# Norms of batches 0 and 1 by halves, and new orders of the engines, in a graph network on one core

## The reference

```
x = norm(x + adj @ (x @ W) + b)                                    # L0
x = norm(x + L1(x))      # ((si + sj' + adj * wr + gb) @ x) @ W + b, si = x.wi, sj = x.wj
x = norm(x + L2(x))      # attention: sigmoid(a_tgt + a_src + be) * mask(adj), times elu(x @ Wi + bi)
for _ in range(5):       # L3: gated unit, h = x at the start
    m  = adj @ h
    z  = sigmoid(m @ W3 + h @ U3 + ..); r = sigmoid(m @ W4 + h @ U3 + ..)
    h  = (1 - z) * h + z * tanh(m @ W5 + (r * h) @ U5 + ..)
x = norm(x + h)
```

## Time and profile before

| | us |
|---|---|
| median of 3 runs (1234.6 to 1240.07) | 1237.77 |
| the profiled execution | 1235.95 |
| its span, first to last instruction | 1234.0 |
| TensorE busy | 1172.3 |
| DVE busy | 927.5 |
| ScalarE busy | 684.7 |
| GpSimd busy | 74.5 |

### The profile page before, as it was taken

One profiled execution on the slowest core, in us unless ns is written; L12 is line 12 of the kernel. 1 busy time (PEld: TensorE's weight loads), 2 busy tenths in 40 slices (PEclk: granted clock), 3 DMA queues, 4 the chain that ended last, 5 costly groups with the idle time before them and its releaser, 6 DMA issues.

```text
span 1234.0 us, 15530 instructions
## 1 busy us (share of the span) xinstructions
PE 1172.3 (95%) x5232; PEld 907.4 (74%) x5232; DVE 927.5 (75%) x2071; ACT 684.7 (55%) x1119; POOL 74.5 (6%) x80
## 2 busy tenths in 40 slices
PE   7979899799999999999999999999999999999995
PEld 5866368577777878877777677887777768788884
DVE  5987986588878886677887886685798788554656
ACT  4336762666566675356567565546457657544443
POOL 0110010000000011001000001000001002000001
PEclk9999999899999999999999999999999999999997
DMA  7222330132222322121232322211332322000001
GB/s 249 87 76 94 102 112 1 34 120 78 94 94 85 95 86 88 41 77 60 92 96 78 128 94 69 69 52 52 104 111 86 111 78 86 18 1 1 1 1 35
DMA packets 92575, 93.66 MB, mean 76 GB/s; under 512 B 9104, under 2 KB 62992, under 8 KB 92496
## 3 DMA queue, kind: packets, MB, share of 16 engines
q1 hardware_dynamic: 92352, 92.27, 23.0%
q0 software_dynamic: 144, 0.40, 0.1%
HBM read 65.35 MB, written 27.29 MB: 75 GB/s over the span
## 4 chain that ended last, share of the span: by engine, by line
PE 58%; DVE 22%; ACT 6%; issue 4%; DMA 4%; SPq 4%; POOL 2%; DVEq 0%; POOLq 0%; ACTq 0%
PE ps L813 33%; PE ps L818 4%; PE ps L820 4%; PE ps L819 4%; PE ps L936 4%; DVE ring L1544 3%; PE ps L831 3%; ACT x L1133 3%; DMA mk<-mask_scratch 2%; SPq L693 2%; DVE tl L1359 2%; DVE hT L1598 1%; DVE v L1595 1%; PE ps L824 1%; DVE ml L1359 1%
## 5 line engine op out<-in xcount | busy, mean ns | idle before, releaser
L813 PE MATMUL ps<-adj_hi,xh 128*128 128x512 f32 x672 | 281.6, 419 | 13.1 <-DVE xl L1359 7.1
L813 PE MATMUL ps<-adj_hi,xl 128*128 128x512 f32 x672 | 263.0, 391 | 0.0
L813 PE MATMUL ps<-adj_lo,xh 128*128 128x512 f32 x672 | 262.5, 391 | 0.0
L813 PEld LDWEIGHTS ps<-adj_hi,xh 128*128 128x128 f32 x672 | 126.7, 189 | 50.4 <-issue 19.0
L813 PEld LDWEIGHTS ps<-adj_lo,xh 128*128 128x128 f32 x672 | 126.8, 189 | 32.6 <-issue 8.9
L813 PEld LDWEIGHTS ps<-adj_hi,xl 128*128 128x128 f32 x672 | 126.4, 188 | 27.3
L1577 DVE TENSOR_TENSOR r<-r,hT 128x512 f32<-128x512 f32 x80 | 53.7, 688 | 76.8 <-ACT r L1271 76.8
L818 PE MATMUL ps<-mh,wh 128*128 128x512 f32 x240 | 101.9, 425 | 6.7 <-DVE ml L1359 5.2
L1544 DVE TENSOR_TENSOR ring<-ring,mk 128x512 f32<-128x512 f32 x128 | 86.9, 685 | 27.2 <-ACT ring L1206 23.9
L1206 ACT ACTIVATE ring<-fh,asn 128x512 f32<-128x512 f32 x96 | 67.3, 719 | 62.6 <-DVE mk L1359 21.5
L1128 ACT ACTIVATE mh<-ps 128x512 fp32r<-128x512 f32 x80 | 47.2, 590 | 92.0 <-PE ps L813 92.0
(11 more groups left out here) (295 smaller groups left out, 2374.2 us busy)
## 6 DMA issues: line engine op xcount, KB each, us to landing
mk<-mask_scratch SPq DMA_DIRECT2D x128, 256.0 KB, 2.8
state_scratch<-v SPq DMA_DIRECT2D x60, 256.0 KB, 2.0
tl<-state_scratch SPq DMA_DIRECT2D x192, 64.0 KB, 2.0
x<-in_x SPq DMA_DIRECT2D x8, 512.0 KB, 4.1
out<-x SPq DMA_DIRECT2D x7, 512.0 KB, 3.2
layer_scratch<-fk SPq DMA_DIRECT2D x12, 256.0 KB, 2.3
fr<-layer_scratch SPq DMA_DIRECT2D x48, 64.0 KB, 2.0
fh<-target_scratch SPq DMA_DIRECT2D x12, 256.0 KB, 3.3
```

What stands on the lines that cost most here:

```text
L813: mm = pe.matmul(dst, a[:, t, :], b[:, t, cut(h)], start=(t == 0 and i == 0), stop=(t == T - 1 and i == 2))
```

## The change

The three norms of batches 0 and 1 are done by halves of four tiles: `v0` becomes `v0a` and `v0b`, `n0` becomes `n0a` and `n0b`, and so on. Each half has its own statistics, power, application and split (`l1a`, `l1b`). TensorE's `m1a` of these batches starts when the first half of xl is there and waits for the second at its fifth tile; `t2a` and `t2b` wait for their own halves. The split for L3 is no longer `start_natural` for batches 0 and 1, but part of `n2a`, `n2b` on ScalarE (`xh3a`, `xh3b`) and two new pieces `l2a`, `l2b` on DVE, and the first state product waits for them by halves. Batches 2 to 7 keep their steps. All five order tables are made anew. The tables of units 2 to 29, of which mainly those of batches 4 and 5 (units 12 to 19) differ, and SP's table are left out here: in the latter, batch 4's `t2`, `f2`, `ax` and `tg` go one unit ahead (unit 12 for 13) and mask loads with them.

```diff
--- before.py
+++ after.py
 "PE": """
-first m0a:0 m0b:0 m0a:1 y0a:0 y0b:0 m0b:1 y0a:1 y0b:1 m0a:2 m0b:2 m1a:0 m1b:0 sums:0 m1a:1 rows:0 y1a:0
-first m1b:1 y1b:0 sums:1 y0a:2 y0b:2 rows:1 y1a:1 y1b:1 t2a:0 t2b:0 pja:0 pjb:0 tha:0 thb:0 tga:0 tgb:0
-first m1a:2 e00:0 e01:0 e02:0 t2a:1 e03:0 m1b:2 e04:0 e05:0 t2b:1 e06:0 e07:0 pja:1 rsa:0 sums:2 rva:0 e10:0
-first e11:0 e12:0 y2a:0 pjb:1 e13:0 e14:0 e15:0 rows:2 y1a:2 tha:1 thb:1 y1b:2 tga:1 e16:0 tgb:1 e17:0 rsb:0
-first rvb:0 e00:1 e01:1 e02:1 e03:1 e04:1 e05:1 e06:1 y2b:0 e07:1 m0a:3 e10:1 e11:1 e12:1 m0b:3 e13:1 e14:1
-first e15:1 e16:1 y0a:3 e17:1 y0b:3 rsa:1 pja:2 pjb:2
-unit0 @2 rsb:1 @5 rva:1 @8 m1a:3 rvb:1 m1b:3 y2a:1 sums:3 y2b:1 rows:3 y1a:3 th0:2 @11 y1b:3 @12 th1:2 @20 th2:2
-unit1 @9 e00:2 @22 e01:2 e02:2 e03:2
+first m0a:0 m0b:0 y0a:0 y0b:0 m0a:1 m0b:1 m1a:0 m1b:0 sums:0 y0a:1 y0b:1 m0a:2 rows:0 y1a:0 m0b:2 y1b:0
+first y0a:2 y0b:2 m1a:1 m1b:1 t2a:0 t2b:0 sums:1 pja:0 pjb:0 rows:1 y1a:1 y1b:1 tha:0 thb:0 tga:0 tgb:0
+first m1a:2 t2a:1 m1b:2 e00:0 e01:0 e02:0 e03:0 sums:2 e04:0 e05:0 e06:0 t2b:1 e07:0 pja:1 rsa:0 rows:2
+first y1a:2 rva:0 e10:0 e11:0 e12:0 pjb:1 y2a:0 y1b:2 e13:0 e14:0 tha:1 e15:0 thb:1 e16:0 tga:1 e17:0 tgb:1
+first rsb:0 rvb:0 e00:1 e01:1 e02:1 e03:1 y2b:0 e04:1 e05:1 e06:1
+unit0 @1 e07:1 @2 m0a:3 e10:1 e11:1 e12:1 m0b:3 e13:1 e14:1 e15:1 e16:1 y0a:3 e17:1 y0b:3 rsa:1 pja:2 pjb:2 @5 rsb:1 @6 th0:2 rva:1 @8 th1:2 m1a:3 rvb:1 m1b:3 y2a:1 sums:3 y2b:1 @10 rows:3 y1a:3 @14 th2:2 y1b:3
+unit1 @12 e00:2 @22 e01:2 e02:2 e03:2
...
 "ACT": """
-first x0:0 x0:1 x0:2 m0a:0 weights:0 m0b:0 m0a:1 m0b:1 n0:0 m0a:2 n0:1 m0b:2 m1a:0 m1b:0 m1a:1 m1b:1 n1:0
-first t2a:0 t2b:0 pja:0 pjb:0 n0:2 tha:0 thb:0 tga:0 n1:1 tgb:0 s00:0 s01:0 s02:0 m1a:2 s03:0 s04:0 s05:0
-first t2a:1 s06:0 m1b:2 s07:0 t2b:1 e07:0 s10:0 s11:0 s12:0 pja:1 rva:0 s13:0 s14:0 s15:0 pjb:1 s16:0 s17:0
-first tha:1 thb:1 tga:1 tgb:1 e17:0 s00:1 s01:1 s02:1 rvb:0 s03:1 s04:1 s05:1 s06:1 n1:2 s07:1 x0:3 e07:1
-first s10:1 s11:1 s12:1 m0a:3 n2:0 s13:1 s14:1 s15:1
-unit0 @0 t2a:2 m0b:3 s16:1 s17:1 t2b:2 e17:1 pja:2 pjb:2 @1 n0:3 @2 rva:1 @4 m1a:3 rvb:1 m1b:3 th0:2 th1:2 n2:1 @9 n1:3 @11 th2:2
-unit1 @1 s00:2 s01:2 @2 q00:2 s02:2 q01:2 @6 s03:2 q02:2 s04:2 s05:2 q03:2 @8 s06:2 @11 q04:2 @16 q05:2 s07:2
+first x0:0 x0:1 x0:2 m0a:0 weights:0 m0b:0 n0a:0 m0a:1 n0b:0 m0b:1 m1a:0 m1b:0 m0a:2 n0a:1 m0b:2 n0b:1 n1a:0
+first n1b:0 m1a:1 m1b:1 t2a:0 t2b:0 n0:2 pja:0 pjb:0 tha:0 thb:0 tga:0 tgb:0 n1a:1 s00:0 s01:0 s02:0 t2a:1
+first m1a:2 m1b:2 s03:0 s04:0 s05:0 n1b:1 s06:0 s07:0 t2b:1 e07:0 s10:0 s11:0 s12:0 pja:1 rva:0 s13:0 s14:0
+first pjb:1 s15:0 s16:0 s17:0 tha:1 thb:1 tga:1 e17:0 tgb:1 s00:1 s01:1 s02:1 rvb:0 s03:1 n2a:0 s04:1 s05:1
+first s06:1 n1:2 s07:1 x0:3 n2b:0 e07:1 s10:1
+unit0 @1 s11:1 s12:1 m0a:3 t2a:2 s13:1 s14:1 s15:1 t2b:2 m0b:3 s16:1 s17:1 e17:1 pja:2 pjb:2 @2 n0:3 rva:1 @4 th0:2 th1:2 rvb:1 m1a:3 m1b:3 n2a:1 n2b:1 th2:2 @9 n1:3 @11 s00:2
+unit1 @1 s01:2 q00:2 s02:2 @2 q01:2 @6 s03:2 q02:2 s04:2 s05:2 q03:2 @8 s06:2 @11 q04:2 @16 q05:2 s07:2
...
 "DVE": """
-first x0:0 x0:1 weights:0 c0:1 c0:0 mask:0 x0:2 y0a:0 y0b:0 mask:1 v0:0 mask:2 y0a:1 y0b:1 mask:3 v0:1 l1:0
-first d1:0 mask:4 l1:1 d1:1 mask:5 c0:2 mask:6 sums:0 mask:7 rows:0 y1a:0 y1b:0 v1:0 sums:1 y0a:2 y0b:2
-first rows:1 v0:2 c2:0 y1a:1 pja:0 pjb:0 y1b:1 v1:1 l1:2 as:0 d1:2 s00:0 s01:0 s02:0 s03:0 s04:0 s05:0 s06:0
-first s07:0 c2:1 s10:0 rsa:0 s11:0 s12:0 pja:1 rva:0 sums:2 s13:0 s14:0 s15:0 y2a:0 pjb:1 rows:2 s16:0 s17:0
-first as:1 y1a:2 rsb:0 s00:1 s01:1 s02:1 y1b:2 v1:2 s03:1 s04:1 s05:1 s06:1 rvb:0 s07:1 x0:3 y2b:0 c0:3 v2:0
-first s10:1 s11:1 s12:1 t2a:2 t2b:2 s13:1 s14:1
-unit0 @0 s15:1 s16:1 s17:1 c2:2 y0a:3 y0b:3 v0:3 rsa:1 pja:2 pjb:2 rsb:1 l1:3 rva:1 @1 d1:3 @2 rvb:1 y2a:1 sums:3 y2b:1 rows:3 v2:1 y1a:3 y1b:3 th0:2 v1:3 th1:2 @9 th2:2
-unit1 @0 ax:2 s00:2 s01:2 q00:2 s02:2 @4 s03:2 q01:2 q02:2 q03:2 @7 s04:2 s05:2 @11 q04:2 @15 q05:2 s06:2
+first x0:0 c0:0 weights:0 x0:1 y0a:0 c0:1 v0a:0 y0b:0 mask:0 v0b:0 l1a:0 mask:1 x0:2 mask:2 l1b:0 d1:0
+first mask:3 c0:2 mask:4 mask:5 sums:0 y0a:1 mask:6 v0a:1 y0b:1 mask:7 rows:0 v0b:1 y1a:0 l1a:1 v1a:0 y1b:0
+first y0a:2 v1b:0 l1b:1 d1:1 y0b:2 v0:2 c2:0 sums:1 rows:1 pja:0 pjb:0 y1a:1 l1:2 v1a:1 as:0 y1b:1 d1:2
+first s00:0 s01:0 s02:0 v1b:1 s03:0 s04:0 s05:0 s06:0 s07:0 sums:2 c2:1 s10:0 rsa:0 s11:0 s12:0 pja:1 rva:0
+first rows:2 s13:0 s14:0 pjb:1 s15:0 s16:0 s17:0 y2a:0 as:1 v2a:0 rsb:0 s00:1 s01:1 s02:1 y1a:2 y1b:2 v1:2
+first s03:1 rvb:0 s04:1 s05:1 y2b:0 s06:1 v2b:0 l2a:0 s07:1 x0:3 c0:3 l2b:0 t2a:2 s10:1 t2b:2 s11:1 s12:1
+first s13:1 s14:1 s15:1 c2:2 s16:1 s17:1 y0a:3 y0b:3 v0:3 rsa:1 pja:2 pjb:2 rsb:1 l1:3 rva:1
+unit0 @2 d1:3 th0:2 rvb:1 th1:2 y2a:1 v2a:1 sums:3 y2b:1 v2b:1 rows:3 l2a:1 l2b:1 y1a:3 y1b:3 th2:2 v1:3 @4 ax:2 @9 s00:2 @13 s01:2 s02:2
+unit1 @1 q00:2 @4 s03:2 q01:2 q02:2 q03:2 @7 s04:2 s05:2 @11 q04:2 @15 q05:2 s06:2
...
 "POOL": """
-first n0:0 n0:1 n1:0 n0:2 n1:1 n1:2 n2:0 n0:3 n2:1 n1:3 n2:2
+first n0a:0 n0b:0 n0a:1 n0b:1 n1a:0 n1b:0 n0:2 n1a:1 n1b:1 n2a:0 n1:2 n2b:0 n0:3 n2a:1 n2b:1 n1:3 n2:2
...
         return {"DVE": norm(a)}
+    if piece[:2] in ("v0", "v1", "v2"):
+        return {"DVE": norm(piece[1:])}
+    if piece in ("n0a", "n0b"):
+        return {"POOL": ("rs0" + a, "nb0" + a), "ACT": ("xn0" + a, "xh1" + a)}
+    if piece in ("n1a", "n1b"):
+        return {"POOL": ("rs1" + a, "nb1" + a), "ACT": ("xn1" + a,)}
+    if piece in ("n2a", "n2b"):
+        return {"POOL": ("rs2" + a, "nb2" + a), "ACT": ("xn2" + a, "xh3" + a)}
+    if piece in ("l1a", "l1b"):
+        return {"DVE": ("xl" + piece[1:],)}
+    if piece in ("l2a", "l2b"):
+        return {"DVE": ("xl3" + a,)}
     if piece == "n0":
...
+HALVED = (0, 1)
 PARTS = (2, 3)
...
-ATTENTION = ("t2", "c2", "pj", "th", "as", "ax", "tg", "rs", "rv", "y2", "v2", "n2")
+ATTENTION = ("t2", "c2", "pj", "th", "as", "ax", "tg", "rs", "rv", "y2", "v2", "n2", "l2")
...
+        def half(name, h, b):
+            return name + "ab"[h] if b in HALVED else name
         def tell(ins, name, b):
...
             return onorms[OUTPUTS[n][0] % 2]
+        def half_tiles(name):
+            return slice(0, T) if len(name) == 2 else slice("ab".index(name[2]) * HT, ("ab".index(name[2]) + 1) * HT)
...
                 f = set_of(name, b)
-                if name in ("n0", "n1", "n2"):
+                if name[:2] in ("n0", "n1", "n2"):
                     _, mv, ve, rs, nb = f["norm"]
-                    seen(pool, "ve" + name[1], b)
-                    tell(pool.tensor_tensor(rs[:, :], ve[:, :], mhalf[:, :], ALU.pow), "rs" + name[1], b)
-                    seen(pool, "rs" + name[1], b)
-                    tell(pool.tensor_tensor(nb[:, :], mv[:, :, 0], rs[:, :], ALU.mult), "nb" + name[1], b)
+                    at = half_tiles(name)
+                    seen(pool, "ve" + name[1:], b)
+                    tell(pool.tensor_tensor(rs[:, at], ve[:, at], mhalf[:, at], ALU.pow), "rs" + name[1:], b)
+                    seen(pool, "rs" + name[1:], b)
+                    tell(pool.tensor_tensor(nb[:, at], mv[:, at, 0], rs[:, at], ALU.mult), "nb" + name[1:], b)
...
                         before_set(name, b)
-                    seen(pe, "xl" + name[1], b)
+                    by_halves = name[1] == "1" and b in HALVED
+                    seen(pe, "xl1a" if by_halves else "xl" + name[1], b)
                     bank = bank_free(name, b)
-                    tell(adj_product(ps[:, bank, :], f["xh"], f["xl"], "ab".index(name[2])), name, b)
+                    tell(adj_product(ps[:, bank, :], f["xh"], f["xl"], "ab".index(name[2]),
+                                     {HT: lambda: seen(pe, "xl1b", b)} if by_halves else {}), name, b)
                 elif name in ("y0a", "y0b", "y1a", "y1b"):
...
                         before_set(name, b)
-                    seen(pe, "xn1", b)
+                    seen(pe, half("xn1", "ab".index(name[2]), b), b)
                     bank = bank_free(name, b)
...
             def state_product(s, h, p, i, prev, breaks):
-                if i == 0:
-                    pe.wait_ge(n_xl[s], p + 1)
+                if i == 0 and p == 0:
+                    seen(pe, "xl3a", s)
+                elif i == 0:
+                    pe.wait_ge(n_xl[s], p)
                 else:
...
                         pe.wait_ge(xl_done, nth(p, i - 1, s, 1))
+                    elif p == 0:
+                        seen(pe, "xl3b", s)
                     if HT in breaks:
...
                     tell(copy(f["m"][:, cut(h)], ps[:, BANKS_A[b][h], :]), "mc" + name[1:], b)
-                elif name in ("n0", "n1", "n2"):
-                    seen(act, "nb" + name[1], b)
-                    tell(norm_apply(x, f["norm"], range(T)), "xn" + name[1], b)
-                    if name != "n0":
-                        return
-                    seen(act, "xn0", b)
-                    tell(copy(f["xh"][:, :, :], x[:, :, :]), "xh1", b)
+                elif name[:2] in ("n0", "n1", "n2"):
```

(46 more changed lines are left out.)

154 lines of the change are left out of this document (77 added, 77 removed).

## The result

| | median of the runs, us | ratio to the kernel before, 95% interval | span of the profiled execution |
|---|---|---|---|
| before | 1238.32 (1234.6 to 1240.07, 4 runs) | | 1234.0 |
| changed | 1246.22 (1243.93 to 1246.68, 4 runs) | 1.0066 (1.0047 to 1.0085) | 1242.1 |

The change makes the kernel slower by about 0.7%; the forecast was 1230.7, faster by 0.6%. First the engines line of the page: TensorE, the same 5232 matmuls, is 4.8 us busier and 3.3 us idler.

A forecast was written before the change was run, and what follows sets the result against it. TensorE, busy 1172.3 of 1234.0 us, was taken to set the pace. A net of -7.1 us from parts 1 to 4 and 0 from the rest gave 1228.9 for the profiled execution, 1230.7 as median; range 1223 to 1242.

The forecast's parts named there:

- Part 1: Start of the kernel: m0a:1 begins only at 30.05 us, a loss of 6.05 us plus 2.0 us for the clock.
- Nothing covers it: Claim at the start that no other TensorE work is ready, so the 6.05 us are lost.
- Part 2: 30 to 97 us: products fill TensorE's waits and pay back the start's loss; m1a:2 at 97.0, net 0.
- Part 3: 97 to 162 us: DVE sets the pace, m0a:3 starts at 162.1, TensorE is 3.6 us behind.
- gain given back: Rival, chance 0.21: DVE idles 6.9 us in 107 to 162 us again, giving 1237.6, no change.
- Part 4: 162 to 232 us: unit 1 starts at 225.5, not 230.82, and at full clock; gain 5.3 + 1.8 = 7.1 us.
- The wait itself goes: Claim that TensorE's 1.59 us wait at about 220 us ends, since the halves stand ahead of the copy mh.
- Part 5: The rest, units 2 to 38: no operation added, effect taken as 0, bounds +3 and -3 us.
- Slower: Rival, chance 0.14: the clock falls in 97 to 162 us; 1244 if 28 of 40 us run at 1.2 GHz.

The follow-up runs named there:

- x7: x2 with two start exchanges: TensorE's m0a:1 ahead of y0a:0 and y0b:0, VectorE's x0:1 ahead of the weights; 1234.69 us, ratio 0.9979.
- x2: The changed kernel with the orders of units 3 to 39 of the kernel before; prologue and units 0 to 2 stay new; 1234.49 us, ratio 0.9972.
- x1: The changed kernel with the orders of units 11 to 39 of the kernel before; prologue and units 0 to 10 stay new; 1235.85 us, ratio 0.9990.
- x11: x2 with VectorE's v1:3 moved behind the split of unit 0's second half and ScalarE's n1:3 to the end of unit 3; 1231.93 us, ratio 0.9952.
- x9: x2 with only TensorE's rows:4, y1a:4, y1b:4 of the new unit 12 set early, and VectorE's rows:4 in unit 11; 1236.80 us, ratio 0.9995.
- x4: The changed kernel with VectorE's y1b:4, v1:4 behind the state's split in unit 12 and ScalarE's n2:5 back in unit 20; 1248.80 us, ratio 1.0094.
- x5: The changed kernel with the state's own work put ahead of fills in units 12 and 20 on VectorE, ScalarE and GpSimd; 1251.75 us, ratio 1.0122.
- x6: x2 with norms 0 and 1 of batches 0 and 1 over whole tiles, norm 2 still by halves; 1254.22 us, ratio 1.0135.

## Why the prediction was wrong

**Part 1, the start.** The trace came out nearly to the tenth (30.05 forecast, 30.52 measured; `t2a:0` 83.7 and 83.78). But "Nothing covers it" failed: x7 took the loss away and the kernel was no faster. The step was the reading that TensorE sets the pace there. VectorE does, busy 26.5 of 28 us in x2 and in x7, so 6.05 us and the clock weren't a price of this order, and the gain of part 2 was not there to pay for them. Two wrong terms made a right sum, and that was luck.

**Part 2.** `m1a:2` was to start at 97.0; it started at 98.32, behind the four matmuls of 95.69, which took 3.62 us at the clock of 0.50 (0.50 from 93 to 98; before also 0.50, and in x2 the same four took 2.04). The wait of 3.09 us went, as said; I took the clock there as full.

**Part 3.** `m0a:3` came at 164.82, 2.7 us after the forecast. VectorE was to work without idle time; it was busy 48.06 of 55 us, as good as the 48.08 of before. This is the rival "gain given back", which I argued against ("most of that was DVE waiting for TensorE's products, now moved out"). What it waited for was not moved out. VectorE's longest wait of the stretch, before and then after, and ScalarE's copy `pm` that stands ahead of its `ring`:

```profile
114.28 0.69 DVE L1544 TENSOR_TENSOR ring<-ring,mk 128x512 f32<-128x512 f32 x1 [3.40 <-ACT ring L1206]
112.50 0.69 DVE L1581 TENSOR_TENSOR ring<-ring,mk 128x512 f32<-128x512 f32 x1 [3.36 <-ACT ring L1238]
110.82 0.60 ACT L1157 ACTIVATE pm<-ps 128x512 f32<-128x512 f32 x1 [4.39 <-PE ps L836]
```

ScalarE waits there for `m1b:2`, a product of batch 2 that stands ahead of s tiles in both orders. In x2, with the same order, this wait was 1.31 us, VectorE was busy 51.07 of the 55 us and `m0a:3` came at 161.28. The clock ahead of it makes the difference: the wait is 1.30 us in x1, where the clock also held at 93 to 98 us, and 3.45 in x11, where it was 0.50. So the forecast of 162.1 was good for an execution whose clock holds at 93 to 98 us. VectorE's added work was below the 5 us I counted: 3.6 in all (931.1 less 927.5).

**Part 4.** The wait of 7.07 us ended, as said. "The wait itself goes" failed for the one ahead of the gates: 1.59 before, 1.71 after. That it was for ScalarE's copy `mh`, behind the whole `n2:1`, was read rightly; VectorE's split `ml` waited for that copy before (first line), and doesn't now (second line).

```profile
219.31 0.69 DVE L1359 TENSOR_TENSOR ml<-ps,mh 128x512 fp32r<-128x512 f32 x1 [1.05 <-ACT mh L1128]
226.90 0.68 DVE L1388 TENSOR_TENSOR ml<-ps,mh 128x512 fp32r<-128x512 f32 x1
```

In the changed kernel the copy ran at 223.92, as soon as its product was there, and `ml` stood behind `v1:3` on VectorE's own queue until 226.90. One holder was taken away and the new order put another in its place. x11 moved `v1:3`, and the wait is gone. The forecast for parts 1 to 4 was -7.1 us. In the eight traces with these orders unit 1 comes 1.1 to 6.0 us earlier, 4.1 in the mean, and x2's ratio says -3.5. The mechanism was right, the size half. In the changed kernel's trace unit 1 came 5.7 us after its forecast (231.19 for 225.5): 2.7 of them are part 3's and 1.7 this wait; the other 1.3 are spread over the stretch.

**Part 5, the step that failed and turned the sign.** "Nothing in the profile singles out a wait that this ends. I take 0, bounds +3": measured +2.2 in units 3 to 10, +8.0 in 10 to 20 and +3.0 behind them. The premise I had read was that TensorE idles only 12 us of 880 there, hence nothing to win. It also means nothing spare to lose: an order with 12 us of idle time in 880 is nearly as good as any, so a new one can hardly be better and is easily worse. That side of the bound was left open by what the row shows, and I closed it at +3 with no price for a wait. I had named the place, units 12 to 15. The rows for a price were there: waits of 1.6 to 2.5 us for ml and ring, and 1.8 us of clock behind one of them (4.54 us where 2.7 is usual). Two such waits with their clock come to some 7 to 9 us, an estimate from these rows, and the block of units 10 to 20 lost 8.0. Its trace shows two fills that left the place where they covered the state's chain, in unit 12 (x9 shows about 3 us for it) and in unit 20 (1.84 us more of waiting, not tested by itself). What the rest is stays open.

**The rivals.** "Given back" happened in part 3 of the changed kernel's trace, less in x2's, and not to the whole (x2 is faster). "Slower" by the clock didn't: the granted clock was 0.97 in that stretch, as before. None of the rivals placed a loss behind unit 3, though most of the changed units are there; part 5 alone had +3 for it.

## What to carry to other kernels

Price each region of a reordering that the title doesn't speak of, and where the bottleneck engine is already busy 98% of a region, set the bound of a new order there from the losing side. Judge two orders by marks that both have and by the sum of the waits, not by one wait: the 6 us at the start were won back in x7 and changed nothing, and in unit 20 the marks showed no loss where a fill had left, because it had been booked just ahead. A fill that bridges a trip through memory belongs to that place, and a piece may be moved back safely only if nothing else waits for it (x11), not if a second chain starts from it (x4, x5).

## What the runs showed of the hardware

The granted clock fell at waits much shorter than the 7.07 us of before, and not every time. With the same orders up to there, the four `tg` matmuls behind waits of 1.65 and 1.25 us took 3.62 us in the changed kernel's trace and 2.04 in x2's; the windows are

```profile
93.00:98.00 5.00, 5.00 (x20) 3.33 (x21) 4.90 (x30) 2.32 (x6) 1.24 (x2) 1.00 0.00 0
```

against 0.50 for the changed kernel above. Up to unit 1 the record has 17.1 us at 0.50 in the changed kernel's trace and 10.2 in x2's; half of the difference, 3.4 us, is lost by it. The two executions of one prologue stand 4.8 us apart there, more than the 3.5 us that the prologue gains. What makes the clock fall in one and not in the other isn't shown. (The Trainium skill, TensorE: Matmul & The Clock Gate, "HAM oscillation — how this bites in real kernels", tells of a clock that falls in waits between groups of products; x6, with 0.53 about its wait of 4.67 us, agrees.)
